# Recurrent part of a fused decoder kernel: low weights and input bias by accumulating DMAs, decay row and positive parts by ScalarE

## The reference

```
x = layernorm(x, ln0_w, ln0_b)
for l in range(4):
    h = layernorm(x, ln1_w[l], ln1_b[l]); hh = time_shift(h)
    k, v = (h*tmk + hh*(1-tmk)) @ Wk.T, (h*tmv + hh*(1-tmv)) @ Wv.T
    sr = sigmoid((h*tmr + hh*(1-tmr)) @ Wr.T)
    # wkv, step by step over the 112 tokens, w = -exp(time_decay), u = time_first
    #   qq = max(pp, u+kk); e1 = exp(pp-qq); e2 = exp(u+kk-qq)
    #   out = (e1*aa + e2*vv) / (e1*bb + e2)
    #   qq2 = max(pp+w, kk); e1b = exp(pp+w-qq2); e2b = exp(kk-qq2)
    #   aa, bb, pp = e1b*aa + e2b*vv, e1b*bb + e2b, qq2
    x = x + (sr * wkv(k, v)) @ Wo.T
    h = layernorm(x, ln2_w[l], ln2_b[l]); hh = time_shift(h)
    kf = square(relu((h*cmk + hh*(1-cmk)) @ Wck.T))          # 256 -> 1024
    x = x + sigmoid((h*cmr + hh*(1-cmr)) @ Wcr.T) * (kf @ Wcv.T)
```

## Time and profile before

| | us |
|---|---|
| median of 3 runs | 1837.8 (1836.41 to 1839.2) |
| the profiled execution | 1835.63 |
| its span | 1833.9 |
| PE busy | 1733.1 (95% of the span) |
| DVE busy | 1242.6 (68%) |
| ACT busy | 978.5 (53%) |
| POOL busy | 3.6 (0%) |

### The profile page before, as it was taken

How to read it: one execution, slowest core, us unless ns; L and a number is a source line. 1 busy time by engine, 2 the same in 40 slices (tenths; PEclk the granted TensorE clock), 3 DMA queues, 4 the chain that set the end, 5 groups by cost and what they waited for, 6 DMA issues and landing times.

```text
span 1833.9 us, 27225 instructions
## 1 busy us (share of the span) xinstructions
PE 1733.1 (95%) x10508; PEld 1517.4 (83%) x10508; DVE 1242.6 (68%) x1918; ACT 978.5 (53%) x1505; POOL 3.6 (0%) x26
## 2 busy tenths in 40 slices
PE   3599999999999998998999999999999999999997
PEld 1378888787888788888899889998999989999896
DVE  7999999999999855888544444444454544444446
ACT  4688898898989873444533333233333332333323
POOL 0000000000000000000000000000000000000000
PEclk9799999999999998999999999999999999999999
DMA  4000010001000002111111011110101001020001
GB/s 143 1 24 18 12 47 18 7 7 61 3 12 29 0 29 89 44 55 45 55 35 35 1 35 35 34 34 0 34 34 34 18 16 34 34 74 0 1 1 41
DMA packets 34702, 56.59 MB, mean 31 GB/s; under 512 B 3030, under 2 KB 20412, under 8 KB 33596
## 3 DMA queue, kind: packets, MB, share of 16 engines
q1 hardware_dynamic: 34620, 55.47, 9.3%
HBM read 51.79 MB, written 3.67 MB: 30 GB/s over the span
## 4 chain that ended last, share of the span: by engine, by line
PE 70%; DVE 24%; ACT 3%; issue 2%; DMA 0%; SPq 0%; ACTq 0%; DVEq 0%
PE fbank L1941 33%; PE fbank L1963 17%; PE pair L842 5%; PE pair L802 4%; PE pair L827 3%; DVE kfl L425 2%; PE proj L1435 2%; PE pair L812 2%; DVE st L272 2%; DVE aa L374 1%; DVE bb L370 1%; DVE pp L356 1%; PE pair L792 1%; PE qbanks L1471 1%; DVE x L413 1%
## 5 line engine op out<-in xcount | busy, mean ns | idle before, releaser
L1763 DVE TENSOR_TENSOR hf<-sil,fbank 128x512 f32<-128x512 f32 (+1 forms) x256 | 158.8, 620 | 479.2 <-PE fbank L1941 407.6
L1868 ACT ACTIVATE sil<-fbank 128x512 f32<-128x512 f32 (+1 forms) x256 | 139.2, 544 | 615.1 <-PE fbank L1941 615.1
L1941 PE MATMUL fbank<-xh,wh 128*128 128x512 f32 (+1 forms) x1024 | 289.9, 364 | 1.2 <-ACT sil L1868 1.2
L1941 PE MATMUL fbank<-xl,wh 128*128 128x512 f32 (+1 forms) x1024 | 289.1, 364 | 0.0
L1941 PE MATMUL fbank<-xh,wl 128*128 128x512 f32 (+1 forms) x1024 | 289.0, 363 | 0.0
L1963 PE MATMUL fbank<-wl,hh 128*128 128x256 f32 x896 | 250.4, 279 | 0.0
L1963 PE MATMUL fbank<-wh,hh 128*128 128x256 f32 x896 | 250.3, 279 | 0.0
L1963 PE MATMUL fbank<-wh,hl 128*128 128x256 f32 x896 | 250.2, 279 | 0.0
L1941 PEld LDWEIGHTS fbank<-xl,wh 128*128 128x128 f32 x1024 | 184.6, 189 | 30.8
L1941 PEld LDWEIGHTS fbank<-xh,wl 128*128 128x128 f32 x1024 | 184.5, 189 | 30.4
L1941 PEld LDWEIGHTS fbank<-xh,wh 128*128 128x128 f32 x1024 | 180.5, 189 | 27.8 <-ACT sil L1868 1.6
(11 more groups left out here) (239 smaller groups left out, 3106.0 us busy)
## 6 DMA issues: line engine op xcount, KB each, us to landing
raw<-in_w_gate SPq DMA_DIRECT2D x16, 512.0 KB, 3.9
raw<-in_w_up SPq DMA_DIRECT2D x16, 512.0 KB, 4.8
raw<-in_w_down SPq DMA_DIRECT2D x16, 512.0 KB, 5.7
raw<-in_w_ck SPq DMA_DIRECT2D x4, 1024.0 KB, 4.7
raw<-in_w_cv SPq DMA_DIRECT2D x4, 1024.0 KB, 4.8
raw<-in_ctx_t SPq DMA_DIRECT2D x4, 750.0 KB, 6.3
ct<-in_ctx_t SPq DMA_DIRECT2D x4, 750.0 KB, 4.9
x<-in_x SPq DMA_DIRECT2D x4, 448.0 KB, 6.8
```

What stands on the lines that cost most here:

```text
L1763: dve.tensor_tensor(hf[i][:, 0:w], sil[i][:, 0:w], banks(e, t, f)[1][:, 0:w], ALU.mult).then_inc(hf_ready, 1)
L1868: act.activation(sil[f % 2][:, 0:w], banks(e, t, f)[0][:, 0:w], ACT.Silu).then_inc(sil_ready, 1)
L1941: ins = pe.matmul(banks(e, t, f)[k][:, 0:w], m[h][:, o:o + P], a[:, b, columns(c)], start=i == 0, stop=i == 3 * CB - 1)
```

## The change

- Low weights. ACT writes the negated weight into the low tile (Copy with scale -1, `minus_weights`, one half at a time), which rounds it to float32r as the high part is; then a DMA issued by POOL adds the float32 weight from HBM onto it (`accum_op=ALU.add`). One half is left to DVE: the second half of `ck` from the second layer on (`late_weights`). PE waits for the DMAs.
- The two halves of `cv` of the first layer and its high part are made at the end of ACT's opening, not in step 0.
- Input bias. For chunks 1 to 3 DVE only scales (`input_scale`), a DMA issued by POOL adds `ln0_b`, broadcast over tokens and sequences, onto `x` in SBUF, and DVE waits for it ahead of the statistics (`biased_stats`). Chunk 1 is normalised by DVE instead of ACT.
- The decay row is written by ACT (`decay_row`).
- Decay arguments. DVE makes one difference `dp = pp[t-1] - k` for both decays, and `dk`. ACT makes the positive parts: `e1b = exp(-relu(exp(td) - dp))`, and `relu(dp + 24 - u)` for `eu`; each Relu is one instruction per half because its bias is per channel.
- In DVE's loop `low_kf(s - 1, 3)` stands ahead of `rsqrt(2, s)`, and `wkv_numerator` behind it.

```diff
+            def add_weights(l, name, i, written):
+                pool.wait_ge(whi_ready[name], written)
+                if sums[name]:
+                    pool.wait_ge(wlo_ready[name], 16 * sums[name])
+                half = slice(i * HALF, (i + 1) * HALF)
+                w = io["w_" + name][l].rearrange("p b c -> p (b c)").bitcast(F32R)
+                pool.dma_start(low[name][LOW[l][i]], w[:, half], accum_op=ALU.add).then_inc(wlo_ready[name], 16)
+                sums[name] += 1
+            def add_bias(m):
+                pool.wait_ge(scaled, m)
+                if m > 1:
+                    pool.wait_ge(biased, 16 * (m - 1))
+                pool.dma_start(x[:, m * G:(m + 1) * G, :],
+                               io["ln0_b"].partition_broadcast(T).unsqueeze(1).broadcast_to([T, G, C]),
+                               accum_op=ALU.add).then_inc(biased, 16)
...
 # vector: wkv_arguments
-                if m % GROUPS == 0:
-                    for b in range(CB):
-                        n = did(dve.tensor_scalar(decay[:, b], reset[:], param(m, b, "w"), None, ALU.add))
-                    after(n)
+                dve.wait_ge(decay_ready, CB * (m // GROUPS + 1))
                 dve.wait_ge(k_out, m + 1)
...
-                dve.tensor_tensor(tokens(dp), at(pp, 0), at(pp, 1), ALU.subtract).then_inc(arg_ready, 1)
+                dve.tensor_tensor(tokens(dp), at(pp, 0), at(kp, 1), ALU.subtract).then_inc(arg_ready, 1)
                 dve.tensor_tensor(tokens(dk), at(kp, 1), at(pp, 1), ALU.subtract).then_inc(arg_ready, 1)
-                for b in range(CB):
-                    dve.scalar_tensor_tensor(du[:, b], kp[:, b, :, 1:T1], param(m, b, "u"),
-                                             pp[:, b, :, 0:T], ALU.add, ALU.subtract).then_inc(arg_ready, 1)
...
 # vector: loop
                 if valid(s + 1):
                     wkv_denominator(s + 1)
-                    wkv_numerator(s + 1)
+                if valid(s - 1):
+                    low_kf(s - 1, 3)
                 if valid(s):
                     rsqrt(2, s)
                     set_shift(2)
-                if valid(s - 1):
-                    low_kf(s - 1, 3)
+                if valid(s + 1):
+                    wkv_numerator(s + 1)
                 if valid(s + 2):
                     mix1(s + 2)
...
 # scalar
+            def minus_weights(l, name, i, used, per):
+                act.wait_ge(stage_in[name], 16 * (l + 1))
...
+                act.activation(low[name][LOW[l][i]], stage[name][:, i * HALF:(i + 1) * HALF], ACT.Copy, scale=-1.0)\
+                    .then_inc(whi_ready[name], 1)
+            def decay_row(m):
+                if m:
+                    act.wait_ge(arg_ready, 2 * m)
+                for b in range(CB):
+                    act.activation(decay[:, b], reset[:], ACT.Identity, bias=param(m, b, "w")).then_inc(decay_ready, 1)
             def wkv_exp(m, what):
+                def over(out, name, scale):
+                    for b in range(CB):
+                        act.activation(out[:, b], dp[:, b], ACT.Relu, bias=param(m, b, name), scale=scale)\
+                            .then_inc(side_ready, 1)
+                per = 2 * CB
                 if what == 0:
...
+                    over(t, "we", -1.0)
+                    act.wait_ge(side_ready, per * m + CB)
+                    act.activation(t, t, ACT.Exp, scale=-1.0).then_inc(exp_ready, 1)
...
                 else:
-                    act.activation(eu[:], rw[m % 2][:], ACT.Relu, bias=most[:], scale=-1.0).then_inc(side_ready, 1)
-                    act.wait_ge(side_ready, m + 1)
+                    over(eu, "mostu", 1.0)
+                    act.wait_ge(side_ready, per * (m + 1))
                     act.activation(eu[:], eu[:], ACT.Exp, bias=most[:], scale=-1.0).then_inc(exp_ready, 1)
...
 # tensor
-                    pe.wait_ge(wlo_ready["cv"], m // GROUPS + 1)
+                    pe.wait_ge(whi_ready["cv"], 3 * (m // GROUPS + 1))
+                    pe.wait_ge(wlo_ready["cv"], 32 * (m // GROUPS) + 16)
...
-                    pe.wait_ge(wlo_ready["ck"], m // GROUPS + 1)
+                    pe.wait_ge(whi_ready["ck"], 2 * (m // GROUPS) + 3)
+                    pe.wait_ge(wlo_ready["ck"], 16 * (m // GROUPS) + 32)
+                    if m >= GROUPS:
+                        pe.wait_ge(late_ready, m // GROUPS)
```

DVE's opening after the change:

```diff
-            set_shift(0)
+            after(normalise(0, chunk(1)))
+            input_scale(1)
             input_stats(2)
-            low_weights(0, "ck", wckh, ck_done, 4)
             mix1(0)
-            input_norm(1)
-            stats(1, chunk(1))
             rsqrt(0, 2)
             set_shift(0)
+            biased_stats(1)
             input_stats(3)
+            input_scale(2)
             wkv_arguments(0)
```

More of the change, by code:

```diff
@@ L302, in input_stats, with input_scale, biased_stats @@
                 dve.wait_ge(x_in[m], 16)
+                if m >= 3:
+                    dve.wait_ge(shift_ready[0], m - 2)
+                stats(0, chunk(m))
+            def input_scale(m):
                 if m >= 2:
[L305 to L311, removed]
+                    dve.wait_ge(xn_ready[0], m - 1)
+                dve.scalar_tensor_tensor(chunk(m), chunk(m), UNIT, ln0w[:].unsqueeze(1).broadcast_to([T, G, C]),
+                                         ALU.mult, ALU.mult).then_inc(scaled, 1)
+            def biased_stats(m):
+                dve.wait_ge(biased, 16 * m)
+                stats(1, chunk(m))
             def difference(m):
@@ L426, in low_kf, with late_weights @@
                     .then_inc(kfl_ready, 1)
[L428 to L444, removed]
+            def late_weights(l):
+                dve.wait_ge(whi_ready["ck"], 2 * l + 3)
+                dve.wait_ge(ck_done, 4 * GROUPS * l)
+                half = slice(HALF, 2 * HALF)
+                dve.tensor_tensor(low["ck"][LOW[l][1]], stage["ck"][:, half], wckh[:, half], ALU.subtract)\
+                    .then_inc(late_ready, 1)
             def gate_channel(m):
@@ L506, in vector @@
             wkv_out(0)
-            input_norm(2)
-            stats(1, chunk(2))
+            biased_stats(2)
             rsqrt(0, 3)
@@ L513, in vector @@
             set_shift(1)
-            input_norm(3)
+            input_scale(3)
             wkv_sums(1)
@@ L546, in vector @@
                     if s and s % GROUPS == 0:
-                        low_weights(s // GROUPS, "ck", wckh, ck_done, 4)
-                    if s % GROUPS == 2 and s + GROUPS < STEPS:
-                        early_weights(s // GROUPS + 1, "ck", 2 * (s // GROUPS) + 1)
+                        late_weights(s // GROUPS)
                 if valid(s + 3):
@@ L647, in high_weights @@
                 act.activation(tile[:], stage[name], ACT.Copy).then_inc(whi_ready[name], 1)
-            def early_weights(l, name, used, per):
+            def minus_weights(l, name, i, used, per):
                 act.wait_ge(stage_in[name], 16 * (l + 1))
-                if l > 1:
-                    act.wait_ge(used, per * GROUPS * (l - 1))
-                act.activation(low[name][LOW[l][0]], stage[name][:, 0:HALF], ACT.Copy).then_inc(early_ready, 1)
-            def wkv_exp(m, what):
-                act.wait_ge(arg_ready, 4 * m + (what + 1 if what < 2 else 4))
-                if what == 0:
-                    for b in range(CB):
-                        act.activation(e1b[:, b, :, 1:T1], dp[:, b], ACT.Exp, bias=param(m, b, "w"))\
-                            .then_inc(exp_ready, 1)
+                free = l if i else l - 1
+                if free > 0:
+                    act.wait_ge(used, per * GROUPS * free)
+                act.activation(low[name][LOW[l][i]], stage[name][:, i * HALF:(i + 1) * HALF], ACT.Copy, scale=-1.0)\
+                    .then_inc(whi_ready[name], 1)
@@ L697, in scalar @@
             norm_out(1, 0, pair[2], "ln1w", "ln1b")
-            normalise(0, 1)
             rsqrt0(0, 2)
+            decay_row(0)
+            normalise(0, 2)
+            rsqrt0(1, 1)
             out(0, "k", kp[:, :, :, 1:T1], k_out)
-            rsqrt0(1, 1)
             out(0, "v", v[:], v_out)
@@ L711, in scalar @@
             reciprocal0(0)
-            normalise(0, 2)
             rsqrt0(0, 3)
@@ L766, in scalar @@
                     out(s + 2, "v", v[:], v_out)
+                    if (s + 2) % GROUPS == 0:
+                        decay_row(s + 2)
                 if valid(s):
```

64 lines of the change are left out of this document (43 added, 21 removed).

## The result

| | before | after |
|---|---|---|
| median of 5 runs, us | 1838.86 (1836.41 to 1839.2) | 1847.09 (1846.02 to 1848.86) |
| ratio, 95% interval | 1 | 1.0052 [1.0041, 1.0062] |
| profiled execution, its span | 1835.63, 1833.9 | 1847.05, 1845.1 |
| first `wo` of step 1 (opening) | 109.29 | 110.28 |
| from there, 13 periods | 513.09 | 520.82 |

The kernel is 8.2 us slower, where 5.3 us faster was predicted. The last four lines split the spans of the two profiled executions at PE's instructions. The opening lost 1.0, the steady stretch 7.7, the last steps gained 0.5, and the part that the change doesn't touch took 3.0 more, 11.2 in all; a remark at the end is on those 3.0.

The account below looks back on a forecast made before the run. In the steady stretch PE was taken as nearly full, with waits for DVE; in the opening DVE was the bound. Opening -4.7, steady -1.0 and end +0.4 gave -5.3 us: 1837.8 to 1832.5, range 1822 to 1841.

Parts of the forecast that it names:

- What bounds the kernel: Steady stretch: PE needs 38.44 us a period, so savings on DVE give back at most 13.4 us.
- What DVE lost: Steady stretch: work removed from DVE, 9.0 us per layer of four steps, 2.2 a step.
- the sum: Steady stretch: waits of 10 x 0.67 + 3 x 1.90 = 12.4 us against 13.4, so 1.0 us gained.
- The ACT term, +1.17: ACT between `hidden(0)` and `hidden(3)`: `e1b` +0.99, `eu` +0.18 us, so `kfh` of pair 3 comes 1.17 later.
- `k` waits until 166.0: 0.67 us: Each steady step: DVE idles for `kfh`, `mix_k`'s first half ends at 166.0, and PE's `k` waits 0.67 us.
- Layer starts: After steps 4, 8, 12: ACT's weight copies make it 1.23 us late, hence 1.90 us of waits against 2.36.
- I take 0: Opening: DVE's wait for chunk 1's bias DMA, bounds 0 to +6.5 us, taken as 0.
- Rival 3: Opening: chunk 1's bias lands late, queued or with DVE blocking POOL's descriptors; 1839.0 us if it takes 13.6; chance 0.09.
- the opening's sum: Opening: DVE's savings bring the `wo` at 109.29 4.7 us earlier, bounds 2.7 to 6.
- The end: Step 15: `low_kf` stands ahead of the rsqrt whose result PE awaits, about +0.4 us.
- Rival 2: Steady stretch: ACT becomes pacer if handoffs or layer copies cost over 0.4 us a step more; loses 5 us; chance 0.11.
- the signs that the prediction gave for them: Next profile: periods over 39.6 us if ACT paces; DVE idle at 28.6 for a DMA if the bias is late.

Follow-up runs that it names:

- low_alone: Kernel before with low weights by DMA and the opening's steps in after's order, all biases by DVE; arguments, decay row, loop order as before: 1829.11 us, ratio 0.9951.
- plain_dma: Kernel after with all of POOL's DMAs as plain copies, without the addition: 1843.55 us (one run).
- bias_first: Kernel after with chunk 1's bias DMA issued by POOL ahead of the first two weight DMAs: 1843.31 us, ratio 1.0030.
- bias1_dve: Kernel after with chunk 1's bias added by DVE ahead of its statistics, the others still by DMA: 1842.66 us, ratio 1.0028.
- The square: Kernel before with new arguments and new loop order, singly and together; 13 periods: neither 513.1 us, order alone 508.4, arguments alone 513.2, both 521.1.
- order_back: Kernel after with DVE's loop order of before (numerator, rsqrt, `low_kf(3)`): 1844.52 us, ratio 1.0038.
- args_back: Kernel after with the decay arguments of before, `eu` too made as before: 1831.57 us, ratio 0.9964.

## Why the prediction was wrong

**What bounds the kernel.** Right: PE's floor is 38.44 (low_alone has periods of 38.44 and 38.45), and DVE alone could give back at most 13.4 us. What DVE lost was nearly right too: 2.2 us a step predicted, and over the 13 periods its busy time went from 496.3 to 469.6, 2.05 a step. One reading of before was off, without effect on the sum: six of its 13 periods have no wait or one of 0.4, not three.

**The ACT term, +1.17.** Right to a few hundredths: `e1b` takes 2.10 to the next instruction's start (2.11 predicted), `eu` 2.20 (2.19), and `kfh` of pair 3 ends 11.24 behind `wo` (11.25).

**"`k` waits until 166.0: 0.67 us".** The mechanism was right and the size wrong. From `kfl` to `mix_k` it is 5.11 us for the 5.0 of the sum, and PE starts 0.83 behind `mix_k`, for which I took 0.60, the pitch of a half. The wait is 0.97.

**The step that was missing.** I followed the path to `k` and stopped. From `mix_k` DVE needs 7.05 us to the end of `gate_channel` (166.43 to 173.48), PE only 6.0 for `k` and `r` after a start 0.83 behind `mix_k`; once `k` waits for DVE, `cr` waits too, for 0.3 us. So the light period is 39.77 and not 39.11, ten times 0.66.

**Layer starts.** The period after step 4 was predicted 40.34 and is 40.11. The number is close by luck: over the floor of 38.44 the sum had 0.67 for the light step and 1.23 for the layer's copies, and it is 1.33 and 0.34. And step 4's own period has 0.55 us that I had not looked for. ACT's `hidden(0)` starts 6.73 us ahead of `wo` (0.41 of it `wo`'s own wait), for 7.09 in the light step, and by the code `wo` needs the bank that ACT's second Relu reads:

```profile
269.23 0.89 ACT L655 ACTIVATE kf<-pair 128x896 f32<-128x896 f32 x1
```

It ends at 270.12, and `wo` starts at 270.22 with 0.41 idle ahead of it. Three such, and 0.3 more in each of the steps 3, 7 and 11, whose cause was not followed: 6.6 + 1.7 + 0.9 less 0.5 at the layer starts is 8.7 us, the distance from the 512.1 of the sum to 520.8. The waits of the stretch come to 21.1 us (520.8 less 499.7), where the sum had 12.4.

**"I take 0" for the bias.** The step that failed in the opening. The time wanted was known (7.1 us), and the nearest row, 6.8, was the lower bound and not the likely value. In its place: issue 2.8 us late (24.49 for 21.7), since POOL waited for a DMA; then 9.4 us to landing. That makes 12.2, and 5.1 of it is seen by DVE. Rival 3 named POOL's wait, and the adding for the 13.6, and was given 0.09; without the adding the wait is 2.54 (plain_dma), in part because POOL then waits less. The mechanism that rival 3 offers, DVE keeping POOL from writing descriptors, is not seen on the bias: from issue to first packet chunk 1 took 2.1 us in bias_first and chunk 2 1.9 in after, where weights took 1.6 in the steady stretch. For POOL's first DMA, which took 5.2 us to its first packet and so held up the bias, it was not tested: DVE and the DMA engines were both busy then. The rest of the opening's sum about held: -4.7 predicted, -3.6 in bias1_dve, which spends 1.25 on an addition that the sum does not have.

**The end.** +0.4 predicted, and it is -0.5 (77.57 for 78.08): the wrong way. No experiment looked at it.

**Rivals and range.** Rivals 2 and 3 came, both at once, and so did the signs that the prediction gave for them: periods over 39.6, and DVE idle at 28.6 for a DMA. Rival 2's trigger, more than 0.4 us a step beyond the sum, was met by the waits at `k` and `cr`, not by the handoffs and copies that it names. They are independent, one in the opening and one in the steady stretch (bias_first and bias1_dve leave the 13 periods at 520.4 and 521.1), so the range should have had their sum, 5 to 6 us each above the forecast, as its upper end; it had room for one. Even that, some 1844, is short of 1847.1. In the spans of the profiled executions the way from -5.3 to +11.2 is 8.7 in the steady stretch, 5.7 in the opening, -0.9 at the end and 3.0 in the part that the change doesn't touch. The forecast also took the edits as one sum. The square shows that they are not: I priced the order as a gain (the wait at `kfl` goes) and ACT's part as +0.67, though the order is what takes away the cover over ACT's 1.17 us.

## What to carry over

When an order is changed so that an engine waits for another earlier in its queue, the other's length can become the pace: price an addition to it at one for one (here 1.18 for 1.19 us), and not by the slack that the old order showed. After a wait is placed at one consumer, walk on to the next consumers of the same engine and to the banks it must get back, for a whole period. In a program that issues DMAs one after the other, put the urgent transfer ahead of any that waits for a transfer. A difference between two single profiles, in the opening above all, should be set against the medians and against parts that the edit cannot reach.

## What the runs showed of the hardware

- In after, POOL's first DMA was issued at 12.70 and its first packet ran at 17.86, 5.2 us later, while the DMA engines were busy throughout with first loads; later ones took 1.6 to 1.9. What held the first was not tried.
- An adding DMA of 512 KB took 3.4 to 3.9 us of packets in after (two of them 5.1 and 5.3), the same without adding 1.6 to 2.4 in plain_dma (the first 3.9). The bias's 448 KB took 6.6 with adding (5.6 in bias1_dve) and 5.65 without: the adding alone accounts for 1.0 us of it at most.
- The part that nothing of the change touches was 3.0 us longer in after's profiled execution. PE's granted clock differs in it. The stretch of 880 to 940 us, before and then after (the value ahead of the last two is the clock):

```profile
880.00:940.00 60.00, 59.70 (x377) 53.43 (x376) 31.48 (x55) 29.21 (x47) 0.00 (x0) 0.97 0.11 36
```

```profile
880.00:940.00 60.00, 57.90 (x330) 50.31 (x329) 32.41 (x60) 32.99 (x52) 0.00 (x0) 0.94 0.14 42
```

The stretch holds a time at the lower level (1.2 GHz), 3.4 us long before and 6.8 after, and the work comes out of it 1.7 us later than before's. The other 1.3 us are lost earlier, between the first projection and the first work of the experts (173.7 us before, 175.0 after), with 10.2 us at the lower level in both. order_back, with 0.97 from 880 to 940 us, has 1133.5 for this part as before has; args_back has 0.97 too, but 0.86 for 0.91 from 700 to 760 us, and 1136.6. All kernels but before and order_back, twelve of the fourteen, have 1135.8 to 1136.7. So the stretches at the lower level fall differently in a part whose code is the same, and as order_back has nearly the whole of the change, the 3.0 us are no cost of it. What sets them apart was not followed further. It fits the two sums: before's profiled execution lies 3.2 us under its median, after's on it, and the spans differ by 11.2, the medians by 8.2; that before's other executions spend the 3 us in this part is not shown.
